# First chunk of a state-space scan without decays, last chunk packed to its real steps

## The reference

```
xn   = x * rsqrt(mean(x^2) + 1e-6) * norm_w
xb, gate = split(xn @ W_in.T)                 # 512 channels each
xc   = silu(causal_conv4(xb) + conv_b)
dt   = soft_clamp(softplus(xc @ W_dt.T + b_dt), 0.001, 0.1)
B_t, C_t = xc @ W_B.T, xc @ W_C.T             # 16 states
dA   = exp(soft_clamp(dt * A, -8, 8))         # tanh, then exp, per channel and state
h    = h * dA + dt * B_t * xc                 # h0 = 0; 512 channels x 16 states x 8 sequences
if t % 10 == 0: h *= min(20 / norm(h), 1)     # norm over all channels and states of a sequence
y    = sum_n(h * C_t) + D * xc
x    = layernorm(2 x + scale * (y * silu(gate)) @ W_out.T)
```

## Time and profile before

| | us |
|---|---|
| median of 3 runs | 2821.68 |
| lowest, highest | 2821.61, 2824.08 |
| the profiled execution's own time | 2822.23 |
| its span | 2820.4 |

### The profile page before, as it was taken

How to read it: one execution, slowest core, us unless ns; L and a number is a source line. 1 busy time by engine, 2 the same in 40 slices (tenths; PEclk the granted TensorE clock), 3 DMA queues, 4 the chain that set the end, 5 groups by cost and what they waited for, 6 DMA issues and landing times. The chain is left out here.

```text
span 2820.4 us, 51549 instructions
## 1 busy us (share of the span) xinstructions
PE 2604.8 (92%) x16812; PEld 2393.3 (85%) x16812; DVE 2401.1 (85%) x3373; ACT 2247.3 (80%) x5011; POOL 2137.4 (76%) x2236
## 2 busy tenths in 40 slices
PE   5799999999999999999999999999999974899992
PEld 4799999999999999999999999999999873677762
DVE  1899999999999999999999999999999995221224
ACT  5999999999999999999999999999999941111113
POOL 0688888888888888888888888888888872434324
PEclk9999999999999999999999999999999996999996
DMA  1222222222222222332322222322222222134226
GB/s 60 64 70 83 75 79 80 76 79 81 73 78 75 79 81 75 79 81 72 81 75 75 83 73 80 81 75 77 80 70 81 71 67 92 38 101 97 64 49 249
DMA packets 153972, 225.72 MB, mean 80 GB/s; under 512 B 46056, under 2 KB 92776, under 8 KB 152552
## 3 DMA queue, kind: packets, MB, share of 16 engines
q1 hardware_dynamic: 131208, 188.98, 23.4%
q0 software_dynamic: 9216, 12.59, 2.6%
q10 hardware_dynamic: 13280, 20.86, 2.2%
HBM read 189.26 MB, written 33.05 MB: 79 GB/s over the span
## 5 line engine op out<-in xcount | busy, mean ns | idle before, releaser
L638 POOL TENSOR_TENSOR H<-H,CB 128x640 f32<-128x640 f32 x832 | 1222.6, 1483 | 207.2 <-DVE H L476 207.1
L476 DVE TENSOR_TENSOR_SCAN H<-DA,PM 128x704 f32<-128x704 f32 x832 | 1316.9, 1603 | 2.2 <-ACT DA L278 2.0
L391 ACT ACTIVATE DA<-DT,SM 128x160 f32<-128x160 f32 x3328 | 1116.1, 424 | 1.5 <-POOL DT L606 0.3
L660 PE MATMUL YB<-H,ID 128*128 128x160 f32 x6656 | 1046.9, 309 | 0.5 <-POOL H L638 0.5
L660 PEld LDWEIGHTS YB<-H,ID 128*128 128x128 f32 x6656 | 985.2, 191 | 16.7 <-issue 11.2
L451 DVE TENSOR_TENSOR PM<-PM,BB 128x640 f32<-128x640 f32 x832 | 677.0, 814 | 1.5 <-DMA BB<-Bd 1.5
L278 ACT ACTIVATE DA<-DA 128x2560 f32<-128x2560 f32 x208 | 485.4, 2334 | 1.7
L666 PE MATMUL PAZ<-XN,WIN 128*128 128x160 f32 x1664 | 254.9, 307 | 3.0 <-DVE VV L536 1.8
L676 PEld LDWEIGHTS PAZ<-XB,CD 128*128 128x128 f32 x1664 | 237.5, 188 | 16.8
L617 POOL TENSOR_TENSOR FC<-SN,HALF 128x4 f32<-128x4 f32 x206 | 233.2, 1132 | 21.7 <-DVE SN L482 7.8
L685 PE MATMUL PAZ<-XC,WDT 128*128 128x160 f32 x1664 | 243.0, 299 | 3.9 <-DVE XC L509 3.9
(11 more groups left out here) (152 smaller groups left out, 2793.5 us busy)
## 6 DMA issues: line engine op xcount, KB each, us to landing
BB<-Bd SPq DMA_DIRECT2D x208, 320.0 KB, 3.5
CB<-Cd SPq DMA_DIRECT2D x208, 320.0 KB, 3.4
W<-in_w ACTq DMA_DIRECT2D x16, 1024.0 KB
XT<-in_xT SPq DMA_DIRECT2D x52, 160.0 KB, 2.2
XR<-in_xp SPq DMA_DIRECT2D x416, 20.0 KB
X2d<-VV SPq DMA_DIRECT2D x416, 20.0 KB
YA<-VV SPq DMA_DIRECT2D x416, 20.0 KB
HI<-YA SPq DMA_DIRECT2D x6, 1024.0 KB, 9.9
```

The source lines that it names most:

```text
L391: eng.activation(DA[:, c0:c0 + 2, :, a, m, 1:11].rearrange("p c b t -> p b c t"), DT[:, j % 2, a].rearrange("p b (c t) -> p b c t", c=2), ...
L476: eng.tensor_tensor_scan(H[:, q % 3, u], a0, DBX(u), 0.0, ALU.mult, ALU.add).then_inc(s_scan, 1)
L638: eng.tensor_tensor(h, h, cb, ALU.mult).then_inc(s_hc, 1)
L660: mm = eng.matmul(yv, ID[:], hv[:, :, :, n, 0:10], start=False, stop=n == 15)
```

## The change

For the first chunk (0): its decays are no longer computed, DA of chunk 0 is zeroed once in the preamble; the 64 tanh of block 0 cover chunk 1 only (128x80), exponentials 0 and 1 of block 0 are gone, n = 2 moves to the end of the iteration before and n = 3 to s = 1; scans of quarters 0 and 1 no longer wait for exponentials.

For the last chunk (103): all its scan data are packed with 4 slots instead of 11 (carry and three steps): scans of 256 elements instead of 704, `mult` of 192 instead of 640, H times C of 256 instead of 640, `y_sum` of 64 columns instead of 160, `z_out` of 64 instead of 160. The 64 tanh of block 51 cover chunk 102 only; those of chunk 103 (`last_tanh`, 64 of 128x24) and its two exponentials (128x768) come in iteration 51, s = 0 to 7. A POOL memset zeroes the packed slots 0 once in iteration 50.

In every other chunk the same elements are addressed as before, but some views are written with one more dimension: the exponentials (`p b (a t)` instead of `p (b a n) t`) and the carry copy (`p u a` instead of `p a`).

```diff
-        PRE_C, PRE_CV, PRE_W, N_PRE = 9, 27, 29, 34
+        PRE_C, PRE_CV, PRE_W, N_PRE = 9, 27, 29, 35
...
+        def cols(c):
+            return 11 if c < NC - 1 else 1 + (L - 1) % 10
+        def rows(c):
+            return min(10, cols(c))
+        def decays(c, g):
+            return DA[:, c % 4, 4 * g:4 * g + 4].rearrange("p b a n t -> p b (a n t)")[:, :, 0:64 * cols(c)]
...
             def exp_a(j, n):
-                v = DA[:, (2 * j + n // 2) % 4, 4 * (n % 2):4 * (n % 2) + 4].rearrange(
-                    "p b a n t -> p (b a n) t")[:, :, 1:11]
+                c = 2 * j + n // 2
+                v = decays(c, n % 2).rearrange("p b (a t) -> p b a t", t=cols(c))[:, :, :, 1:cols(c)]
                 eng.activation(v, v, ACT.Exp, scale=16.0).then_inc(s_da, 1)
+            def last_tanh(n0, n1):
+                j, c = NB - 1, NC - 1
+                k = cols(c)
+                for n in range(n0, n1):
+                    a, m = n // 16, n % 16
+                    eng.activation(
+                        DA[:, c % 4].rearrange("p b a n t -> p b (a n t)")[:, :, 0:64 * k].rearrange(
+                            "p b (a n t) -> p b a n t", a=4, n=16)[:, :, a, m, 1:k],
+                        DT[:, j % 2, a, :, 10:9 + k], ACT.Tanh, scale=AS[:, a, m:m + 1]).then_inc(s_z64, 1)
...
-                    if s in (1, 3, 5) and ok(i):
+                    if s in (1, 3, 5) and 0 < i < NB - 1:
                         exp_a(i, (s + 1) // 2)
+                    if i == 0 and s == 1:
+                        exp_a(0, 3)
+                    if i == NB - 1 and s < 8:
+                        if s == 1:
+                            exp_a(i, 1)
+                        last_tanh(8 * s, 8 * s + 8)
+                        if s == 7:
+                            eng.wait_ge(s_z64, 64 * (NB + 1))
+                            exp_a(i, 2)
+                            exp_a(i, 3)
...
+                            k0, k1 = int(j == 0), 2 - int(j == NB - 1)
                             eng.activation(
-                                DA[:, c0:c0 + 2, :, a, m, 1:11].rearrange("p c b t -> p b c t"),
-                                DT[:, j % 2, a].rearrange("p b (c t) -> p b c t", c=2), ACT.Tanh,
+                                DA[:, c0 + k0:c0 + k1, :, a, m, 1:11].rearrange("p c b t -> p b c t"),
+                                DT[:, j % 2, a].rearrange("p b (c t) -> p b c t", c=2)[:, :, k0:k1], ACT.Tanh,
                                 scale=AS[:, a, m:m + 1]).then_inc(s_z64, 1)
...
-                        exp_a(i + 1, 0)
+                        exp_a(i + 1, 0 if i >= 0 else 2)
...
-            eng.memset(DA[:, :, :, :, :, 0:1].rearrange("p c b a n t -> p (c b a n) t"), 0.0).then_inc(s_pre, 1)
+            eng.memset(DA[:, 0].rearrange("p b a n t -> p (b a n t)"), 0.0).then_inc(s_pre, 1)
+            eng.memset(DA[:, 1:4, :, :, :, 0:1].rearrange("p c b a n t -> p (c b a n) t"), 0.0).then_inc(s_pre, 1)
...
             def scan(q, u):
...
                 if u == 0:
-                    eng.wait_ge(s_da, q + 1)
+                    if q >= 2:
+                        eng.wait_ge(s_da, q - 1)
+                    if c == NC - 1:
+                        eng.wait_ge(s_slot, 1)
...
-                eng.tensor_tensor_scan(H[:, q % 3, u], a0, DBX(u), 0.0, ALU.mult, ALU.add).then_inc(s_scan, 1)
+                n = 64 * cols(c)
+                eng.tensor_tensor_scan(H[:, q % 3, u, 0:n], decays(c, g)[:, u], DBX(u)[:, 0:n], 0.0, ALU.mult,
+                                       ALU.add).then_inc(s_scan, 1)
...
+                    if i == NB - 2 and s == 0:      # on POOL
+                        k = cols(NC - 1)
+                        eng.memset(DA[:, (NC - 1) % 4].rearrange("p b a n t -> p b (a n t)")[:, :, 0:64 * k].rearrange(
+                            "p b (a t) -> p b a t", t=k)[:, :, :, 0], 0.0).then_inc(s_slot, 1)
```

More of the change, by code:

```diff
@@ L99, in ssm_phase @@
             sem("bcs"), sem("sp"), sem("dth"), sem("tg"), sem("z64"), sem("da"), sem("x2t"), sem("hsq"))
-        s_halo, s_sgh, s_dx, s_dxh, s_hc = sem("halo"), sem("sgh"), sem("dx"), sem("dxh"), sem("hc")
+        s_halo, s_sgh, s_dx, s_dxh, s_hc, s_slot = sem("halo"), sem("sgh"), sem("dx"), sem("dxh"), sem("hc"), sem("slot")
         s_min, s_dt, s_xn, s_pow, s_fac, s_car = (
@@ L450, in mult @@
                     eng.wait_ge(s_scan, 4 * q + u - 1)
+                k = cols(c)
                 eng.tensor_tensor(
-                    DBX(u).rearrange("p (a n t) -> p a n t", a=4, n=16)[:, :, :, 1:11],
-                    U(c)[:, :, 4 * g + u, :].unsqueeze(2).to_broadcast([128, 4, 16, 10]),
-                    BB[:, q % 2, :, u, :].unsqueeze(1).to_broadcast([128, 4, 16, 10]), ALU.mult).then_inc(s_m1, 1)
+                    DBX(u)[:, 0:64 * k].rearrange("p (a n t) -> p a n t", a=4, n=16)[:, :, :, 1:k],
+                    U(c)[:, :, 4 * g + u, 0:k - 1].unsqueeze(2).to_broadcast([128, 4, 16, k - 1]),
+                    BB[:, q % 2, :, u, 0:k - 1].unsqueeze(1).to_broadcast([128, 4, 16, k - 1]), ALU.mult).then_inc(s_m1, 1)
             def carry(q, u):
-                o = PM[:, 640:640 + 2 * CH].rearrange("p (a t) -> p a t", t=11)[:, :, 0]
+                k = cols(q // 2)
+                o = PM[:, 640:640 + 2 * CH].rearrange("p (u n) -> p u n", u=2)[:, :, 0:64 * k].rearrange(
+                    "p u (a t) -> p u a t", t=k)[:, :, :, 0]
                 if 4 * q + u >= 2:
@@ L465, in carry @@
                         eng.wait_ge(s_car, q - 1)
-                    eng.tensor_copy(o, CAR[:, u:u + 2].rearrange("p u a -> p (u a)")).then_inc(s_ca, 1)
+                    eng.tensor_copy(o, CAR[:, u:u + 2]).then_inc(s_ca, 1)
             def scan(q, u):
@@ L470, in scan @@
                 eng.wait_ge(s_ca, 2 * q + u // 2 + 1)
+                c, g = q // 2, q % 2
                 if u == 0:
-                    eng.wait_ge(s_da, q + 1)
+                    if q >= 2:
+                        eng.wait_ge(s_da, q - 1)
+                    if c == NC - 1:
+                        eng.wait_ge(s_slot, 1)
                     if q >= 3:
                         eng.wait_ge(s_ys, 3 * (q - 2))
-                a0 = DA[:, (q // 2) % 4, 4 * (q % 2) + u].rearrange("p a n t -> p (a n t)")
-                eng.tensor_tensor_scan(H[:, q % 3, u], a0, DBX(u), 0.0, ALU.mult, ALU.add).then_inc(s_scan, 1)
+                n = 64 * cols(c)
+                eng.tensor_tensor_scan(H[:, q % 3, u, 0:n], decays(c, g)[:, u], DBX(u)[:, 0:n], 0.0, ALU.mult,
+                                       ALU.add).then_inc(s_scan, 1)
             def norm_sum(q):
@@ L487, in z_out @@
                 j, cc = c // 2, c % 2
-                o = vw(Z[:, :, 4 * g:4 * g + 4, 10 * cc:10 * cc + 10])
-                yv = YP(q).rearrange("p (u a t) -> p u a t", u=4, a=4)
+                k = rows(c)
+                o = vw(Z[:, :, 4 * g:4 * g + 4, 10 * cc:10 * cc + k])
+                yv = YP(q).rearrange("p (u a t) -> p u a t", u=4, a=4)[:, :, :, 0:k]
                 eng.wait_ge(s_ys, 3 * (q + 1))
@@ L494, in z_out @@
                 eng.wait_ge(s_sg, j + 1)
-                eng.tensor_tensor(o, yv, vw(SG[:, j % 2, :, 4 * g:4 * g + 4, 10 * cc:10 * cc + 10]),
+                eng.tensor_tensor(o, yv, vw(SG[:, j % 2, :, 4 * g:4 * g + 4, 10 * cc:10 * cc + k]),
                                   ALU.mult).then_inc(s_z, 1)
@@ L631, in gpsimd_program @@
                                           ALU.mult).then_inc(s_xn, 1)
+                    if i == NB - 2 and s == 0:
+                        k = cols(NC - 1)
+                        eng.memset(DA[:, (NC - 1) % 4].rearrange("p b a n t -> p b (a n t)")[:, :, 0:64 * k].rearrange(
+                            "p b (a t) -> p b a t", t=k)[:, :, :, 0], 0.0).then_inc(s_slot, 1)
                     if live:
-                        h = H[:, q % 3, u].rearrange("p (a n t) -> p a n t", a=4, n=16)[:, :, :, 0:10]
-                        cb = CB[:, q % 2, :, u, :].unsqueeze(1).to_broadcast([128, 4, 16, 10])
+                        k, n = cols(q // 2), rows(q // 2)
+                        h = H[:, q % 3, u, 0:64 * k].rearrange("p (a n t) -> p a n t", a=4, n=16)[:, :, :, 0:n]
+                        cb = CB[:, q % 2, :, u, 0:n].unsqueeze(1).to_broadcast([128, 4, 16, n])
                         if u == 0:
@@ L643, in y_sum @@
                     return
-                hv = H[:, q % 3].rearrange("p u (a n t) -> p u a n t", a=4, n=16)
-                yv = YP(q).rearrange("p (u a t) -> p u a t", u=4, a=4)
+                k, w = cols(q // 2), rows(q // 2)
+                hv = H[:, q % 3, :, 0:64 * k].rearrange("p u (a n t) -> p u a n t", a=4, n=16)
+                yv = YP(q).rearrange("p (u a t) -> p u a t", u=4, a=4)[:, :, :, 0:w]
                 if n0 == 0:
@@ L655, in y_sum @@
                         eng.wait_ge(s_red, min(q, NQ - 2))
-                    eng.matmul(yv, ID[:], DX[:, j % 2, :, 4 * g:4 * g + 4, 10 * cc:10 * cc + 10].rearrange(
```

(3 more changed lines are left out.)

## The result

| | before | after |
|---|---|---|
| median, us (5 runs each, together on one chip) | 2821.68 | 2808.12 |
| lowest, highest | 2820.95, 2824.08 | 2807.19, 2808.52 |
| profiled execution's own time | 2822.23 | 2807.19 |
| its span | 2820.4 | 2805.4 |

The ratio is 0.995 (95% interval 0.9935 to 0.9964): 13.56 us faster. The forecast of 2805.0 is 3.1 us too low. So of the 3.1 us 1.8 (2807.19 against 2805.4) are the sum's and 1.5 are where the two profiled runs lie among the others; the forecast had been rounded up by 0.1, which gives the rest.

What follows compares the result with a forecast made beforehand. DVE and ACT, in step, were taken to bound the middle, so only the ends count: start 5.5 plus end 11.3 makes 16.8 us, from 2822.23 to 2805.4, median said as 2805. Range: 2801 to 2813 us.

Steps and rivals of the forecast that it cites:

- Middle untouched, only the ends count: Middle blocks: DVE and ACT both bound them and nothing there changes; the gain is what the two ends lose.
- Start 5.5: First blocks: less tanh and exponential work on ACT, which sets the start, saves 5.5 us by block 1's XC.
- The walk: Start, step by step: ACT's and DVE's savings followed to block 1's XC; 5.5 us, or 3.2 to 7.9.
- ACT is 5.55 earlier: Block 0, from ACT's squares after DVE's scans: ACT runs 5.55 us earlier, which sets the gain at block 1's XC.
- Decisive size 0.26 for a half tanh: Tanh of 80 elements on ACT: 0.26 us from start to start instead of 0.32, bounds 0.16 and 0.32.
- End until the first LGS copy, 8.9: End, quarter 206 to the LGS copy of 2328.11: shorter packed work brings that copy to 2319.2, 8.9 us earlier.
- the late carry: End, after quarter 206: the carry, behind the norm's sum and POOL, comes late and DVE idles 1.1 us.
- The packed exponentials: ACT, iteration 51: the last chunk's two exponentials end about 2.5 us before the first packed scan wants them.
- PE is then the long one ... SP is free 0.6 us before that copy: End, up to the last LGS copy: PE's chain decides, SP's DMA issues finish 0.6 us sooner; copy 11.3 us earlier.
- rival 3: End: its gain is hidden by SP or ACT's late packed tanh; start and 2 us remain, 2814; 6%.
- Packed `y_sum` 3.1 us: PE at the end: each packed sum over states at 64 columns takes 3.1 us, 0.09 an instruction.
- Rival 4: Packed end: PE falls to 1.2 GHz, some 4 us less gain, 2809; 12%.

Runs made afterwards that it cites:

- e_queue: The kernel after, with the last blocks' router logits and YA stores moved from SP's queue to ACT's; 2805.71 us (0.9945).
- e_warmall: The kernel after, with unused PE matmuls: 24, 16, 28 and 50 before iterations -4, -2, -1 and 0, 13 before iteration 1's norm sum; 2799.10 us.
- e_same: The kernel after again, unchanged, run beside the other kernels on the same chip; 2807.73 us (0.995).
- e_fullt: The kernel after, with all 64 tanh of block 0 at 128x160 again and the first scan waiting for them; 2811.63 us (one run).

## Why the prediction was right, and where it was off

- **Middle untouched, only the ends count**: right. From XC of block 1 (5.58 earlier) to quarter 206 (5.80) the gain changes by 0.2 us.
- **Start 5.5**: right in sum, 5.6 to 5.8, by errors that cancel, which is luck. The walk took PE's durations from the trace as fixed. In block 0 PE's clock came back sooner and gave 1.1; in block 1 it fell and took 1.6. Some 0.5 us came before 52.84, where the walk had put nothing (the tanh L344 starts at 52.36). The term "ACT is 5.55 earlier" was a difference of ACT's own work, but what ACT waits for had changed its speed.
- **Decisive size 0.26 for a half tanh**: right; its bounds 0.16 and 0.32 carried the range.
- **End until the first LGS copy, 8.9**: right, 8.8, with quarter 206, the late carry and each packed size. The packed exponentials were ready 1.35 us before the first packed scan, where 2.5 had been worked out.
- **"PE is then the long one ... SP is free 0.6 us before that copy"**: this step failed. The end gave 8.8 to the load of LG (9.2 with the second phase) instead of 11.3. I asked when SP was free for its next issues, and not who waits for what it had issued: VV of block 51 overwrites the buffer that the DMAs of block 50 read, so it waits for the last of them to land, 1.3 us behind the issue. With that wait the prediction's own numbers give 8.9: its last issue ends at 2330.3, VV starts at 2331.6 and the LGS copy comes 1.66 us later, at 2333.2 instead of 2342.13. That the issues last as long as before held in this trace (10.96 for 10.92 us), but not in others: X2d and YA together took 6.5 to 8.0. This is what rival 3 said of SP (6%), as a loss of 2.5 us and not of the whole end.
- **Packed `y_sum` 3.1 us**: mis-sized. It took 3.73, or 0.117 us per instruction by the division that gave 0.149; 0.09 had been taken. The Trainium skill (TensorE: Matmul & The Clock Gate, LDWEIGHTS) had been weighed there and set aside for the row of the transposes at 0.067; its 107 ns for 128 columns of weights, by estimate 3.6 us for the sum, comes close to what the trace shows. The row that I took instead was of another shape (80 rows of weights); why that one follows at 0.067 no run here shows. In after the 1.2 us for both sums cost nothing, since VV waited for SP; with SP out of the way, in e_queue, the two LGS copies are 12.2 us apart where 11.7 were forecast.
- **Rival 4, PE's clock in the packed end**: did not come; both sums took 3.73, with a granted clock of 1.00 from 2310 to 2320.

## What to carry to other kernels

Before a gain is carried over an engine's own queue to the next landmark, list everything that the landmark's instruction waits for, buffers read by DMAs first, and give each its new end. A wait that a trace puts down to one engine can belong to a second one that ends a tenth of a microsecond later. Where an engine that bounds the kernel waits for PE after a quiet stretch of PE, look at the granted clock: unused matmuls in five such stretches cost nothing that the traces show and brought XC of block 1 7.5 us earlier here, over half of what the change itself gave. The medians have 8.6 (e_warmall against e_same); SP's shorter issues add to that figure, and the longer second phase of e_warmall takes from it.

## What the runs showed of the hardware

- A stretch of PE's work that follows a quiet one of 3.16 us ran at 1.2 GHz in after (1.23 us for what takes 0.71), and with 26 instructions of unused matmuls in the quiet it ran at 2.4; yet 3.24 us of quiet in the kernel before had no such effect, and in e_fullt, after 3.15 us of quiet, the same four matmuls took 0.71 and only the projection behind them was slow (4.01 us for 2.34).
- 32 float32 matmul instructions with 128 x 128 weights took 4.77 us at 160 columns and 3.73 us at 64: 60% fewer columns save 22%.
- Eight small DMA issues on SP took 3.54 to 5.04 us for the X2d store of block 50, alike in two runs of the same kernel (5.04, 4.97) and different between kernels. Why stays open. From the end of the last issue to the start of the instruction that waited for its landing it was 1.26 or 1.27 us each time.
